# One weight array with one table value per block, and a last stage with its sums split over three engines

## What is computed

```python
probs = jax.nn.softmax(x @ gate_w, axis=-1)
w, sel = jax.lax.top_k(probs, K)                      # K = 8 of 32 experts
w = w / jnp.sum(w, axis=-1, keepdims=True)
...
g = jnp.einsum('ech,ehi->eci', xg, w_gate)            # [32, C, 256] x [32, 256, 96]
u = jnp.einsum('ech,ehi->eci', xg, w_up)
y = jnp.einsum('eci,eih->ech', jax.nn.silu(g) * u, w_down).reshape(E * C, H)
out = jnp.zeros((T + 1, H), x.dtype).at[t_slot].add(w_slot[:, None] * y)
...
x = _layernorm(x + _L0_ffn_ref(x, ...), axis=-1)
```

## Time and profile before

| what | value |
|---|---|
| median of 3 runs | 681.29 us (678.33 to 681.3) |
| profiled execution | 684.91 us, its span 683.1 us |
| PE busy | 537.2 us, 79% of the span |
| DVE, ACT, POOL busy | 383.3, 359.8, 347.8 us |
| granted clock of PE, mean | 0.934 |
| expert rounds | 19, from about 356 to 614 us of the span |
| last stage, from the first load of results | 617.5 to 683.1 us |

### The profile page before, as it was taken

The page is one execution under the profiler, slowest core; times in us unless marked ns, Lnnn a source line. Parts: engine busy times, 40 slices in busy tenths (PEclk is TensorE's granted clock), DMA queues, the critical chain, the costliest instruction groups (busy, mean ns, idle before and its releaser), DMA issues.

```text
span 683.1 us, 18720 instructions
## 1 busy us (share of the span) xinstructions
PE 537.2 (79%) x5130; PEld 413.6 (61%) x5131; DVE 383.3 (56%) x1761; ACT 359.8 (53%) x1253; POOL 347.8 (51%) x541
## 2 busy tenths in 40 slices
PE   2788788888888888884039998998898989885994
PEld 2455455555555554542028887887788878884883
DVE  1457777777777777764114454544444544452773
ACT  2466676666666666762015665665565656560111
POOL 6352445455555545545406776676676767670000
PEclk9999999999999999995559999999999999997998
DMA  9999999222222111222864555555555555558981
GB/s 199 274 260 374 349 339 339 86 77 77 77 77 77 67 67 73 85 77 88 283 207 144 178 168 162 164 176 155 167 160 153 175 158 165 153 157 327 419 324 48
DMA packets 83457, 121.35 MB, mean 178 GB/s; under 512 B 13779, under 2 KB 73181, under 8 KB 81376
## 3 DMA queue, kind: packets, MB, share of 16 engines
q1 hardware_dynamic: 62880, 77.74, 37.6%
q0 software_dynamic: 13824, 37.78, 15.5%
q10 hardware_dynamic: 6720, 5.41, 2.6%
HBM read 56.07 MB, written 69.01 MB: 183 GB/s over the span
## 4 chain that ended last, share of the span: by engine, by line
PE 59%; DVE 14%; ACT 10%; issue 10%; DMA 3%; ACTq 2%; POOL 1%; SPq 0%; DVEq 0%; POOLq 0%
PE bank L721 15%; PE bank L738 10%; PE bank L711 6%; ACT pr L792 5%; PE bank L762 4%; PE bank L543 3%; PE bank L533 3%; PE bank L731 3%; PE bank L593 2%; PE bank L672 2%; PE bank L766 2%; DVE nmax L981 2%; ACTq L289 2%; PE bank L630 2%; ACT prT L798 2%
## 5 line engine op out<-in xcount | busy, mean ns | idle before, releaser
L502 POOL DMA_INDIRECT results<-ys,wcol x152 | 149.8, 986 | 26.0 <-POOL pscrap L491 21.2
L480 POOL DMA_INDIRECT queues<-x,xidx x128 | 126.1, 985 | 39.9 <-issue 39.9
L721 PE MATMUL bank<-wgu,xtT 128*128 x616 | 130.8, 337 | 0.1
L1165 DVE SCALAR_TENSOR_TENSOR tg<-th,bank 128x96 f32<-128x96 f32 x154 | 39.2, 254 | 119.3 <-ACT th L883 119.3
L711 PE MATMUL bank<-ident,xt 128*128 128x128 f32 x310 | 64.7, 291 | 52.3 <-issue 28.8
L721 PEld LDWEIGHTS bank<-wgu,xtT 128*128 128x128 f32 x616 | 100.8, 198 | 0.5 <-issue 0.4
L792 ACT ACTIVATE pr<-bank,nmax 128x128 f32<-128x128 f32 x256 | 90.7, 370 | 19.6 <-DVE nmax L981 19.2
L711 PEld LDWEIGHTS bank<-ident,xt 128*128 128x128 f32 x310 | 59.6, 199 | 68.1 <-issue 37.2
L890 ACT ACTIVATE ys<-bank,wcol 128x256 f32<-128x256 f32 x152 | 72.0, 474 | 46.0 <-PE bank L738 46.0
L738 PE MATMUL bank<-wd,hT 96*128 x304 | 93.4, 389 | 0.0
L875 ACT COPY xtT<-bank 128x256 f32<-128x256 f32 x155 | 56.6, 365 | 39.4 <-PE bank L711 36.7
(11 more groups left out here) (180 smaller groups left out, 934.6 us busy)
## 6 DMA issues: line engine op xcount, KB each, us to landing
xt<-queues SPq DMA_DIRECT2D x162, 160.0 KB, 2.2
results<-zeros SPq DMA_DIRECT2D x16, 1024.0 KB
wgu<-results SPq DMA_DIRECT2D x16, 1024.0 KB, 9.0
queues<-zeros SPq DMA_DIRECT2D x34, 160.0 KB, 5.5
wgu<-in_L_ffn_w_gate SPq DMA_DIRECT2D x4, 768.0 KB, 11.9
wgu<-in_L_ffn_w_up SPq DMA_DIRECT2D x4, 768.0 KB, 13.7
wd<-in_L_ffn_w_down SPq DMA_DIRECT2D x4, 768.0 KB, 13.5
queues<-zeros ACTq DMA_DIRECT2D x16, 160.0 KB
```

Of the source, the lines that this page charges most:

```text
L480: pool.indirect_dma_start(xg, bass.IndirectOffsetOnAxis(ap=xidx[:, par, k:k + 1], axis=0), x2[:, par, :], None, bounds_check=last_row, oob ...
L502: pool.indirect_dma_start(yr, bass.IndirectOffsetOnAxis(ap=wcol[:, u, 1:2], axis=0), ys[:, u, :], None, bounds_check=last_y, oob_is_err=Fa ...
L721: ins = pe.matmul(bank[2 + u % 2][:, 0:2 * INTER].rearrange("p (g i) -> p g i", g=2), xtT[:, u % 2, kk, :], wgu[:, bass.ds(e, 4 * INTER)]. ...
```

## The change

- `wgu` and `wd` become one array `wall` with 640 columns an expert: 384 of gate and up, 256 of down (in 96 of its 128 partitions). One table value, the expert times 640, addresses both. At a round's head PE loads ten entries of `tab_g`, for the blocks t to t+9, in place of eight and eight; `tab_d` is gone.
- The last stage has ten result slots in place of six.
- POOL adds planes 4 and 5 (`pair_z`), PE sums planes 6 and 7, `pair_z`, `pair_y` and the residual, in eight PSUM banks in place of four.
- The inverse root is taken for groups of 4, 4, 4, 2 and 2 batches (`LAST`), bias and scale for a group in one operation each.
- ACT issues two of a batch's four stores, SP the other two, in turn with its remaining loads.

```diff
-YB = 6
+YB = 10
+LAST = (4, 4, 4, 2, 2)
+GU = 2 * 2 * INTER
+WX = GU + D
...
+        def store(eng, b, first, last):
+
+            for g in range(first, last):
+                t0 = first_token(g)
+                eng.dma_start(out[b, t0:t0 + DIL * (GR - 1) + 1:DIL, :],
+                              fin[GR * g:GR * (g + 1), b % 4, :]).then_inc(stored[b % 4], 16)
...
-            for b in range(NB):
-
-                if b >= YB:
-                    sp.wait_ge(peC, b - YB + 1)
+            def load_results(b):
...
+            for b in range(YB):
+                load_results(b)
+            for b in range(NB):
+                if b + YB < NB:
+                    sp.wait_ge(peC, b + 1)
+                    load_results(b + YB)
+                sp.wait_ge(actC, b + 1)
+                store(sp, b, 2, NG)
...
+            for b in range(NB):
+                yb = combined(b % YB)
+                pool.wait_ge(y_in[b % YB], 16 * (b // YB + 1))
+                if b >= 4:
+                    pool.wait_ge(peC, b - 3)
+                pool.tensor_tensor(pair_z[:, b % 4, :], yb[:, 4 * D:5 * D], yb[:, 5 * D:6 * D], ALU.add
+                                   ).then_inc(pooled, 1)
...
-                e_gu = neighbours(ET.PE, tab_g[0:1, bass.ds(j * UN + UN, UN)], (NE - 1) * 4 * INTER)
-                e_down = neighbours(ET.PE, tab_d[0:1, bass.ds(j * UN, UN)], (NE - 1) * D)
+                e = neighbours(ET.PE, tab_g[0:1, bass.ds(j * UN + LEAD, UN + 2)], (NE - 1) * WX)
...
-                ps = bank[b % 4]
-                if b >= 4:
-                    pe.wait_ge(actC, b - 3)
+                ps = bank[b % 8]
+                if b >= 8:
+                    pe.wait_ge(actC, b - 7)
                 pe.wait_ge(y_in[b % YB], 16 * (b // YB + 1))
-                for n in range(4, TOPK):
+                for n in range(6, TOPK):
                     pe.matmul(ps[:, 0:D], ident[:, :], combined(b % YB)[:, n * D:(n + 1) * D],
-                              start=(n == 4), stop=False)
+                              start=(n == 6), stop=False)
+                pe.wait_ge(pooled, b + 1)
+                pe.matmul(ps[:, 0:D], ident[:, :], pair_z[:, b % 4, :], start=False, stop=False)
                 pe.wait_ge(paired, b + 1)
...
+            b = 0
+            for c, n in enumerate(LAST):
+                for i in range(n):
+                    if b >= 4:
+                        act.wait_ge(stored[b % 4], 16 * NG * (b // 4))
+                    act.wait_ge(dveC[c].sem, dveC[c].at(0, "r"))
+                    act.activation(fin[:, b % 4, :], bank[b % 8][:, 0:D], ACT.Identity,
+                                   bias=nb[:, c % 2, i:i + 1], scale=rs[:, c % 2, i:i + 1]).then_inc(actC, 1)
+                    b += 1
+                    act.wait_ge(actC, b)
+                    store(act, b - 1, 0, 2)
...
+            added = 2
+            for c, n in enumerate(LAST):
...
+                for i in range(n):
+                    if added < NB:
+                        pairs_of(added)
+                        added += 1
+                    dve.wait_ge(peC, first + i + 1)
+                    stats(dveC[c], 0, (f"s{i}",), i, bank[(first + i) % 8][:, 0:D])
+                dve.wait_ge(s, C(f"a{n - 1}"))
+                root(dveC[c], 0, 0, n)
+                if c >= 2:
+                    dve.wait_ge(actC, ends[c - 2])
```

More of the change, by code:

```diff
@@ L1 @@
+import itertools
 from contextlib import ExitStack
@@ L165, in build @@
         scrap = sb("scrap", [1, 2 + 2 * UN])
[L166 to L173, removed]
+        st6 = sb("st6", [P, 4, 6])
+        mv = sb("mv", [P, 4, 2])
+        ve = sb("ve", [P, 4])
+        nh = sb("nh", [P, 4])
+        half = sb("half", [P, 4], I32)
+        ry = sb("ry", [P, 4])
+        rt = sb("rt", [P, 4])
+        rz = sb("rz", [P, 4])
         spare = sb("spare", [1, 2])
         pscrap = sb("pscrap", [1, 1])
-        nb = sb("nb", [P, 4])
-        rs = sb("rs", [P, 4])
+        nb = sb("nb", [P, 2, 4])
+        rs = sb("rs", [P, 2, 4])
         took = sb("took", [NE, 1])
@@ L206, in build @@
         pair_y = sb("pair_y", [P, 4, 2 * D])
+        pair_z = sb("pair_z", [P, 4, D])
         x_in = [sem("x_in0"), sem("x_in1")]
@@ L242, in build @@
         actC = sem("actC")
-        dveC = Steps(sem("dveC"), f"s0 a0 s1 a1 {ROOT} b0 b1 r0 r1")
+        pooled = sem("pooled")
+        dveC = [Steps(sem(f"dveC{c}"), " ".join(f"s{i} a{i}" for i in range(n)) + f" {ROOT} b r")
+                for c, n in enumerate(LAST)]
         scattered = [sem(f"scattered{k}") for k in range(2)]
@@ L310, in _ @@
             for e in range(0, NE, 8):
[L311 to L314, removed]
+                sp.dma_start(wall_v[:, e:e + 8, 0:GU // 2], gate_v[:, e:e + 8, :]).then_inc(experts_loaded, 16)
+                sp.dma_start(wall_v[:, e:e + 8, GU // 2:GU], up_v[:, e:e + 8, :]).then_inc(experts_loaded, 16)
+                sp.dma_start(wall_v[0:INTER, e:e + 8, GU:WX], down_v[:, e:e + 8, :]).then_inc(experts_loaded, 16)
             sp.wait_ge(consts, N_CONST)
@@ L742, in _ @@
                 block_T(t, t, 0)
-            for t, e in zip((0, 1), neighbours(ET.PE, tab_g[0:1, 0:UN], (NE - 1) * 4 * INTER)[LEAD:]):
+            for t, e in zip((0, 1), neighbours(ET.PE, tab_g[0:1, LEAD:UN], (NE - 1) * WX)):
                 gu(t, t, e)
@@ L1137, in tables @@
                 dve.wait_ge(s, H("fe"))
-                for tab, first, times, plus in ((tab_g, LEAD, 4 * INTER, 0), (tab_w, LEAD, 1, D), (tab_d, 0, D, 0)):
+                for tab, first, times, plus in ((tab_g, LEAD, WX, 0), (tab_w, LEAD, 1, D)):
                     dve.tensor_scalar(tab[0:1, first:first + TAB], tab_f[0:1, 0, :], float(times), float(plus),
@@ L1203, in pairs_of @@
                 dve.tensor_tensor(pair_y[:, b % 4, :], yb[:, 0:2 * D], yb[:, 2 * D:4 * D], ALU.add).then_inc(paired, 1)
+            ends = list(itertools.accumulate(LAST))
             for b in range(2):
                 pairs_of(b)
[L1207 to L1216, removed]
-                if c >= 2:
[L1218 to L1225, removed]
+            added = 2
+            for c, n in enumerate(LAST):
+                C, s = (lambda name: dveC[c].at(0, name)), dveC[c].sem
+                first = ends[c] - n
+                for i in range(n):
[6 more added lines that the diff above has]
+                root(dveC[c], 0, 0, n)
+                if c >= 2:
+                    dve.wait_ge(actC, ends[c - 2])
+                dve.scalar_tensor_tensor(nb[:, c % 2, 0:n], mv[:, 0:n, 0:1].rearrange("p n o -> p (n o)"), -1.0,
+                                         rz[:, 0:n], ALU.mult, ALU.mult).then_inc(s, 1)
+                dve.tensor_copy(rs[:, c % 2, 0:n], rz[:, 0:n]).then_inc(s, 1)
 _INS = ["x", "ctx_512", "L0_xattn_Wq", "L0_xattn_Wkv_expand", "L0_xattn_Wout", "L0_ffn_gate_w",
```

18 lines of the change are left out of this document (8 added, 10 removed).

## The result

The changed kernel takes 710.88 us (707.84 to 711.49), the kernel before 680.56 us beside it: 1.0442 times as long, with an interval of 1.0402 to 1.0482. The forecast was 659.5 us. The loss is in the expert rounds alone.

What follows compares the result with a forecast made beforehand. TensorE was taken to bound both stages, with lookup holes at round heads. Gains of 12.9 + 4.5 + 7.1 = 24.5 us cut the span from 683.1 to 658.6, plus 1.8 around it 660.4; median forecast 659.5 us, range 654 to 667.

Steps and rivals of the forecast that it cites:

- Expert rounds: Head of each expert round: one lookup of ten replaces two of eight, 0.68 us in 19 rounds, -12.9 us.
- Added: two entries in the remaining lookup ... from above each costs an eighth of 0.593: Expert rounds' lookup: two more entries cost between nothing and 0.15 us a round; 0.05 was taken.
- Granted clock: Expert rounds: with holes of about 0.8 us, the three low-clock rounds of 1.5 us extra vanish, -4.5 us.
- The one array: Expert rounds' products: weights lying in one array cost nothing, since the moving rows are as long as before.
- Tail sums, data, root and stores: Last stage: six TensorE products a batch, not seven, and stores split over two queues; stage ends at 676.0, not 683.1, -7.1 us.
- Entries are dear: Rival, expert rounds: added entries cost more or low-clock rounds stay; rounds gain 8.4 to 10, 662 to 666 us; chance 0.17.
- The hole is not the lookup: Rival, expert rounds: the jump itself costs most of 1.5 us, so only the tail gains, 674 us; chance 0.05.
- Slower: Rival, last stage: TensorE waits each batch for POOL's sum or the load, its clock falls to 1.2 GHz, 699 us; chance 0.02.
- the 17.4 forecast: Expert rounds: the gain of 12.9 us from the lookup and 4.5 us from the granted clock taken together.
- the bound of 14.3 us: Expert rounds: the largest gain allowed for replacing two lookups by one, beside a smallest of 8.4 us.
- 2.95 us: Last stage, rival that data bounds the tail: time of each load next to stores; stage gains 4 us, 663 us; chance 0.12.
- 657.5 with the loop's upper bound: Rival, last stage: stores land at once, no queue behind loads, 1.9 us more gained, 657.5 us, or 655; chance 0.12.

Runs made afterwards that it cites:

- two_eights: The changed kernel with two lookups of eight entries and a second table again, starts at multiples of eight: 671.54 us, 0.9866 of the kernel before.
- ten_aligned: The changed kernel with its table shifted by two entries, so each list of ten starts at 8j + 8: 665.93 us, 0.9777 of the kernel before.
- three_pieces: ten_aligned with its lookup cut into three of four entries, one behind the round's first transposes, two inside the round: 649.55 us, 0.9523 of the kernel before.
- split_8_2: The changed kernel with its ten entries fetched by two lookups, eight and two, both from starts off a multiple of four: 722.70 us, 1.0628 of the kernel before.
- stores_on_act: ten_aligned with all four stores of a batch issued by ScalarE again, SyncE only loading: 675.36 us, 0.9898 of the kernel before.
- ten_aligned_again: ten_aligned unchanged, run on a slow chip as the base for other runs there: 803.10 us, 0.9814 of the kernel before.

## Why the prediction was wrong

- **Expert rounds, "Added: two entries in the remaining lookup ... from above each costs an eighth of 0.593".** This step failed. It priced ten entries by eight others and took the price to hang on their number. It hangs first on where the list starts. The change's `LEAD` of 6 makes it start at 8j + 6, and each of the ten entries costs as much as if it were fetched apart: 2.68 us in place of 0.65, 23.4 us of longer holes where 12.9 of shorter ones were forecast. The start stood in the diff (`j * UN + LEAD` for `j * UN + UN`) and was not looked at; every lookup of the kernel before starts at a multiple of eight entries, so its price could not have been read there, only doubted. Aligned, the ten take 1.15 us: my upper bound of 0.15 us for two entries was too low by a factor of three even so. The holes then shrink by 6.3 us (28.8 to 22.5), not by 12.9, and the rounds are 4.2 us shorter than with two lookups of eight.
- **The price of a lookup, by the Trainium skill and by the runs.** The Trainium skill's page "DMA: Bandwidth & Descriptors" (section "Latency and other measured facts") has a floor of about 600 ns for a lookup. Here one entry took 0.298 to 0.313 us and four 0.340, so the measurement is below it; the 593 ns that the prediction took for agreement were the price of eight entries. The Trainium skill's page "Runtime: NRT & Kernel Launch" (section "Instruction fetch mechanics") has some 200 ns for each register loaded from main memory. I set it against 8 entries in 593 ns and dropped it. On-chip lookups from a start off a multiple of four cost 250 ns an entry (2.495 us for ten), a quarter above its figure, and aligned ones 75 ns (0.597 us for eight). Its figure was the right warning, for a case that it doesn't name.
- **Granted clock.** The sign came out wrong because the holes grew: behind holes of 2.6 to 3.1 us, 9 of the 17 rounds after the first ran at a clock of 0.89 to 0.90, where before it was 3 rounds. TensorE's busy time for the same products rose by 10.0 us. It fell by 5.0, 3.3 and 5.1 us in two_eights, ten_aligned and three_pieces, with holes of 1.5, 1.2 and 0.3. But two_eights has the holes of the kernel before, one of 1.83 us among them, and no low-clock round after its first. So the 4.5 us can come and go by chance from execution to execution, and no run shows that shorter holes bring them; that much longer ones cost them, the change and split_8_2 (249.03 us busy) show. Nor does the length of a hole alone decide: one of 2.96 us was followed by a round at 1.00 and one of 2.62 by a round at 0.89.
- **The one array** at nothing: right, by the rounds of two_eights.
- **Tail sums, data, root and stores: -7.1 us.** Measured -6.8 (65.6 to 58.8). TensorE ended 49.9 us after the first load (48.9 forecast). Stores landed late, 8.95 and 10.03 us after issue where the chain shows them; ScalarE waited 7.5 us for its slots, worked off seven batches at the end as forecast, and came to the last one 55.55 us after the first load (55.5 forecast). The size was right and so was most of the path, but the reason for the late stores was not: the prediction had SyncE's half late, because it stands behind loads in SyncE's queue. ScalarE's half has no load in front of it and landed later still (10.0 us against 8.5 at batch 5), and in stores_on_act, where SyncE stores nothing, stores are as late. They are late on either queue while loads run; why is open. That this term came out is luck. What the stage loses without one part is another sum, and doesn't add up to 6.8: without two issuers of stores 7.8 us (more than the 1.8 at the end, since all late batches profit), without POOL's sum 4.4 to 5.1 (6.6 at TensorE's end, 6.9 forecast), without the ten slots 17.3, without the root for four nothing.
- **Rivals.** "Entries are dear" pointed at the right place with less than a tenth of the price: 0.15 us a round, measured 2.0. "The hole is not the lookup" is out, since the holes follow the lookup's length in every run. "Slower" had the wrong mechanism: TensorE did not wait for POOL or loads after its first batch. With the lookup's start put right the kernel takes 665.93 us, inside the range that was forecast, partly by luck: in the profile its rounds gain 9.6 us of the 17.4 forecast, its last stage 7.0 of 7.1.
- **Slips in the sums.** The midpoint of tab_d's 0.593 and 0.832 is 0.71 us, not 0.64; the bound of 14.3 us is given without its terms; one load and one batch's stores (2.53 and 0.46) make 2.99 us, not 2.95; and 657.5 with the loop's upper bound is 656.1, not 655. None of them changes what failed.

## What to carry to other kernels

Let every list of table entries (four bytes each here) that TensorE's sequencer looks up start at a multiple of 16 bytes from the array's start, and its length be a multiple of four entries. Each entry left over, and each entry of a list that starts elsewhere, cost a quarter of a microsecond. Put lookups behind products that are already issued, in pieces if needed, and not at the head of a loop: that was worth more (16 us, on the chips of the first runs) than halving their number (6 us). The other engines were not probed with such starts, so for them the rule is a guess. When two instructions are merged into one, compare all of the operand, its start too, not only its size.

## What the runs showed of the hardware

- One lookup: 1 entry 0.30 us, 4 aligned 0.34, 8 aligned 0.60, 16 aligned 1.11; 8 from the entries 5, 6, 7, 9 and 10 1.93 to 2.10 us, with no return to the fast form when the list crosses a multiple of four.
- Two chips on which the same kernel takes 818 us where others take 680. By ten_aligned_again against ten_aligned, the first block lands 102 us later (451.8 for 349.9) and the expert rounds are 32 us longer, while the last stage takes the same 59 us. In the attention stage the granted clock is 0.85 against 0.98 and a 128x512 product takes 0.721 us against 0.614; in the rounds the clock is 0.97 on both, and a transpose takes 0.289 against 0.288. The cause is open.
